# Scattering token numbers in place of token rows in a mixture-of-experts sort that runs beside attention

## The reference, cut to what matters

```python
xn = layernorm(x)
s  = attention(xn)                        # 16 heads of 16, bias by distance (ALiBi)
# mixture of experts, each token goes to 2 of 8 experts
scores   = sigmoid(xn @ router.T)
topk_idx = the two chosen experts, topk_w = their normalised scores
y_e      = (silu(xn @ w_gate[e]) * (xn @ w_up[e])) @ w_down[e]
routed   = sum over the two chosen e of topk_w * y_e
g = silu(routed + shared expert)
out = x + s * g
```

## Time and profile before

| what | us |
|---|---|
| median of 3 runs | 2485.53 |
| lowest and highest of them | 2479.53, 2488.43 |
| the profiled execution | 2477.84 |
| its span from first to last instruction | 2476.1 |
| tokens stage in the span | 0 to 371 |
| attend stage, sort part | 445 to 653 |
| attend stage, expert tiles | 704 to 2043 |
| attend stage, mix | 2047 to 2290 |
| deliver stage | from 2340 |

### The profile page before, as it was taken

How to read it: one execution, slowest core, us unless ns; L and a number is a source line. 1 busy time by engine, 2 the same in 40 slices (tenths; PEclk the granted TensorE clock), 3 DMA queues, 4 the chain that set the end, 5 groups by cost and what they waited for, 6 DMA issues and landing times. The chain is left out here.

```text
span 2476.1 us, 41361 instructions
## 1 busy us (share of the span) xinstructions
PE 2051.5 (83%) x15921; PEld 723.3 (29%) x15922; DVE 1007.1 (41%) x2375; ACT 1792.6 (72%) x2080; POOL 549.8 (22%) x577
## 2 busy tenths in 40 slices
PE   4688875676799999999999999999999998788565
PEld 2345542111122224222222332222224221111154
DVE  6676656411133335333333443333335332444255
ACT  3444444566798888888888888888888887888610
POOL 1222220566401111111111111111111104555022
PEclk9888886878899999999999999999999998989888
DMA  9766664554323325332333443233335323433296
GB/s 305 232 212 215 214 204 110 147 155 143 116 74 92 98 78 142 96 86 84 95 96 85 111 114 98 79 94 92 91 87 136 102 63 81 120 103 105 56 285 219
DMA packets 212584, 316.75 MB, mean 128 GB/s; under 512 B 81744, under 2 KB 156112, under 8 KB 212128
## 3 DMA queue, kind: packets, MB, share of 16 engines
q1 hardware_dynamic: 172064, 197.63, 29.1%
q0 software_dynamic: 31872, 108.03, 14.4%
q10 hardware_dynamic: 8448, 8.39, 1.0%
HBM read 196.25 MB, written 125.83 MB: 130 GB/s over the span
## 5 line engine op out<-in xcount | busy, mean ns | idle before, releaser
L1203 ACT ACTIVATE probs_att<-SC_att 128x1024 f32<-128x1024 f32 (+10 forms) x1776 | 1578.0, 956 | 289.0 <-PE SC_att L1093 205.5
L1116 PE MATMUL O_att<-probs_att,V_att 128*32 128x512 f32 (+6 forms) x8192 | 954.1, 535 | 17.1 <-DVE probs_att L1229 15.8
L1093 PE MATMUL SC_att<-Q_att,K_att 64*128 64x512 f16 (+6 forms) x4332 | 654.9, 341 | 241.1 <-ACT probs_att L1203 168.5
L1229 DVE TENSOR_TENSOR probs_att<-probs_att,decay_att 128x128 f32<-128x128 f32 x1024 | 293.5, 291 | 1094.6 <-ACT probs_att L1203 1012.3
L1093 PEld LDWEIGHTS SC_att<-Q_att,K_att 64*128 64x128 f16 (+1 forms) x4332 | 183.2, 94 | 1138.9 <-ACT probs_att L1203 850.2
L1116 PEld LDWEIGHTS O_att<-probs_att,V_att 128*32 128x32 f32 x8192 | 167.6, 110 | 248.6 <-issue 202.3
L1038 POOL DMA_DIRECT2D ys<-ys_att x72 | 51.5, 716 | 743.3 <-DVE ys_att L1276 743.3
L1033 POOL DMA_DIRECT2D xs_att<-xs x72 | 53.3, 740 | 445.6 <-PE TY_att L1137 431.8
L1045 POOL DMA_INDIRECT rows_in_att<-ys,place x128 | 125.5, 981 | 117.5 <-DVE gate_all L1285 83.5
L581 POOL TENSOR_TENSOR parts_tok<-qk_tok,parts_tok 128x512 f16<-128x512 f32 x64 | 78.6, 1230 | 247.0 <-ACT parts_tok L601 242.3
L1023 POOL DMA_INDIRECT xs<-rows_in_att,place x128 | 124.4, 972 | 39.6 <-issue 39.6
(11 more groups left out here) (153 smaller groups left out, 1333.2 us busy)
## 6 DMA issues: line engine op xcount, KB each, us to landing
K_att<-k_stack SPq DMA_DIRECT2D x128, 256.0 KB
Q_att<-q_stack SPq DMA_DIRECT2D x128, 256.0 KB
xs<-zero_tok SPq DMA_DIRECT2D x36, 512.0 KB, 3.8
xs_att<-xs POOLq DMA_DIRECT2D x72, 256.0 KB, 3.2
ys<-ys_att POOLq DMA_DIRECT2D x72, 256.0 KB, 2.6
k_stack<-parts_tok SPq DMA_DIRECT2D x96, 128.0 KB
q_stack<-parts_tok SPq DMA_DIRECT2D x96, 128.0 KB
x_raw_tok<-in_x SPq DMA_DIRECT2D x16, 512.0 KB, 5.7
```

Source lines behind the costliest of these rows:

```text
L1093: mm = pe.matmul(SC[:, c % SLOTS, at:at + x1 - x0], K[par][side or 0][rows, k * P:(k + 1) * P], Q[par][rows, x0:x1], start=True, stop=True)
L1116: mm = pe.matmul(O[VW * g:VW * (g + 1), par, col:col + width * len(mine)], V[par][:, k, :], spans[:, j0:j0 + BPB * (len(mine) - 1) + 1:BPB ...
L1203: nc.scalar.activation(probs[chunk.step % DEPTH][:, chunk.base:chunk.base + chunk.width], SC[:, c % SLOTS, start:start + chunk.width], ACT ...
L1229: v.tensor_tensor(diag, diag, decay[:, chunk.head, :], ALU.mult).then_inc(faded, 1)
```

## The change

`xs` is gone. In its place stands `order`, one 4-byte number for each of the 18432 slots, filled with zeros by one DMA of 72 KB. POOL scatters token numbers (`ids`, a constant, held as floats) into `order` with the same 128 indirect DMAs by the same `place`, one after the other with no load and no wait between them. When all have landed it loads `order` as 72 rows of 256 and waits on `order_ready`. PE turns the two halves with two transposes at chunk 252 of batch 0 (`ORDER_AT`), and DVE turns the result into integers (`row_of`). Each `load_tile` then gathers its 256 rows straight from `xn` with two indirect DMAs of 128 rows. The first tile moves from 50 to 56 per cent of batch 0 (chunk 264), with the last where it was. The slots that only fill up a list all name token 0; their results aren't read.

```diff
-FF_FROM, FF_TO = 50, 340
+FF_FROM, FF_TO = 56, 340
+ORDER_AT = 252
+        "ids": np.arange(B * S, dtype=np.float32).reshape(NBLK * TT, P).T,
-        zero = r.sb("zero", [P, 1024])
+        zero = r.sb("zero", [P, SLOTS_IN // P])
...
                 sp.wait_ge(zeroed, 1)
+                sp.dma_start(keep["order"].rearrange("(p k) o -> p (k o)", p=P), zero[:]).then_inc(zeros_out, 16)
                 for j in range(NBLK):
-                    for n in range(j * NZ // NBLK, (j + 1) * NZ // NBLK):
-                        sp.dma_start(keep["xs"].rearrange("(p k) d -> p (k d)", p=P)[:, 1024 * n:1024 * (n + 1)], zero[:]).then_inc(zeros_out, 16)
...
-                def sort_rows(j):
-                    pool.wait_ge(rows_loaded[j % 2], 16 * (j // 2 + 1))
-                    for t in range(TT):
-                        for n in range(2):
-                            nc.gpsimd.indirect_dma_start(keep["xs"], index(keep["place"][:, n, j * TT + t:j * TT + t + 1]),
-                                                         rows_in[:, j % 2, t, :], None).then_inc(sorted_out[j % 2], 16)
+                def sort_tile(t):
+                    for n in range(2):
+                        nc.gpsimd.indirect_dma_start(keep["order"], index(keep["place"][:, n, t:t + 1]), ids[:, t:t + 1], None).then_inc(sorted_out, 16)
...
-                    src = keep["xs"][i * TILE_IN:(i + 1) * TILE_IN, :].rearrange("(t p) d -> p t d", p=P)
-                    pool.dma_start(xs[:, i % 2], src).then_inc(xs_in[i % 2], 16)
+                    for t in range(2):
+                        nc.gpsimd.indirect_dma_start(xs[:, i % 2, t, :], None, keep["xn"], index(row_of[:, t, i:i + 1])).then_inc(xs_in[i % 2], 16)
...
-                load_rows(0)
                 pool.wait_ge(routed, 1)
-                for j in range(NBLK):
-                    if j + 1 < NBLK:
-                        if j > 0:
-                            pool.wait_ge(sorted_out[(j + 1) % 2], 16 * 2 * TT * ((j + 1) // 2))
-                        load_rows(j + 1)
-                    sort_rows(j)
-                for n in range(2):
-                    pool.wait_ge(sorted_out[n], 16 * 2 * TT * (NBLK // 2))
+                for t in range(NT):
+                    sort_tile(t)
+                pool.wait_ge(sorted_out, 16 * 2 * NT)
+                pool.dma_start(order[:], keep["order"].rearrange("(i k) o -> i (k o)", k=TILE_IN)).then_inc(order_in, 16)
+                pool.wait_ge(order_ready, 1)
                 load_tile(0)
                 load_tile(1)
...
+                def turn_order():
+                    pe.wait_ge(loaded, 64)
+                    pe.wait_ge(order_in, 16)
+                    for t in range(2):
+                        mm = pe.transpose(TY[:, t * TILES_IN:(t + 1) * TILES_IN], order[:, t * P:(t + 1) * P], ident[0:TILES_IN, 0:TILES_IN])
+                    mm.then_inc(order_turned, 1)
...
                                 prefixes()
+                            if b == 0 and c == ORDER_AT:
+                                turn_order()
...
+                def take_order():
+                    dve.wait_ge(order_turned, 1)
+                    v.tensor_copy(row_of[:].rearrange("p t i -> p (t i)"), TY[:, 0:2 * TILES_IN]).then_inc(order_ready, 1)
...
+                        if b == 0 and c == ORDER_AT:
+                            take_order()
```

More of the change, by code:

```diff
@@ L394, in tokens_stage @@
         ALL_LOADED = 16 * len(loads)
-        NZ = SLOTS_IN * D // 1024 // P
         x_rows = a["x"].rearrange("b s d -> (b s) d")
@@ L467, in _ @@
                 sp.wait_ge(w_stored, 32 * E)
-                sp.wait_ge(zeros_out, 16 * NZ)
+                sp.wait_ge(zeros_out, 16)
                 sp.wait_ge(shift_out, 16 * NBLK)
@@ L853, in attend_stage @@
         O = r.ps("O", [P, 2, TB])
-        rows_in = r.sb("rows_in", [P, 2, TT, D])
+        fetched = r.sb("fetched", [P, 4, 2, D])
+        ids = r.sb("ids", [P, NT])
+        order = r.sb("order", [TILES_IN, TILE_IN])
+        row_of = r.sb("row_of", [P, 2, TILES_IN], I32)
         ident = r.sb("ident", [P, P])
@@ L913, in attend_stage @@
         step, counted = r.sem("step"), r.sem("counted")
-        rows_loaded = [r.sem(f"rows_loaded{n}") for n in range(2)]
-        sorted_out = [r.sem(f"sorted_out{n}") for n in range(2)]
+        sorted_out, order_in, order_turned, order_ready = r.sem("sorted_out"), r.sem("order_in"), r.sem("order_turned"), r.sem("order_ready")
         w_in = [r.sem(f"w_in{n}") for n in range(3)]
@@ L928, in attend_stage @@
         per_choice = lambda t: t.unsqueeze(2).broadcast_to([P, NT, E])
-        route_loads = [(lower[:], a["lower"]), (starts[:], a["starts"]), (lane[:], a["lane"]),
+        route_loads = [(lower[:], a["lower"]), (starts[:], a["starts"]), (lane[:], a["lane"]), (ids[:], a["ids"]),
                        (earlier[:].bitcast(U16), a["earlier"]), (every[:].bitcast(U16), a["every"]),
@@ L935, in attend_stage @@
         weighted = keep["weighted"].rearrange("(n r) s -> n r s", r=HD)
-        pairs = rows_in[:].rearrange("p n t d -> p (n t d)").rearrange("p (n k d) -> p n k d", n=4, d=D)
+        pairs = fetched[:]
         PRODUCTS = [(c, wp, xp) for c in range(DC) for wp, xp in ((0, 0), (0, 1), (1, 0))]
@@ L1011, in _ @@
             def _(pool):
-                rows_of = lambda j: keep["xn"][j * TB:(j + 1) * TB, :].rearrange("(t p) d -> p t d", p=P)
                 index = lambda ap: bass.IndirectOffsetOnAxis(ap=ap, axis=0)
-                def load_rows(j):
-                    pool.dma_start(rows_in[:, j % 2], rows_of(j)).then_inc(rows_loaded[j % 2], 16)
-                def sort_rows(j):
-                    pool.wait_ge(rows_loaded[j % 2], 16 * (j // 2 + 1))
-                    for t in range(TT):
-                        for n in range(2):
-                            nc.gpsimd.indirect_dma_start(keep["xs"], index(keep["place"][:, n, j * TT + t:j * TT + t + 1]),
-                                                         rows_in[:, j % 2, t, :], None).then_inc(sorted_out[j % 2], 16)
+                def sort_tile(t):
+                    for n in range(2):
+                        nc.gpsimd.indirect_dma_start(keep["order"], index(keep["place"][:, n, t:t + 1]), ids[:, t:t + 1], None).then_inc(sorted_out, 16)
                 def load_tile(i):
@@ L1130, in turn_tile @@
                         pe.wait_ge(loaded, 64)
-                    pe.wait_ge(xs_in[i % 2], 16 * (i // 2 + 1))
+                    pe.wait_ge(xs_in[i % 2], 32 * (i // 2 + 1))
                     if i > 0:
@@ L2663, in build @@
             "xn": scratch("xn", (B * S, D), F32),
-            "xs": scratch("xs", (SLOTS_IN, D), F32),
+            "order": scratch("order", (SLOTS_IN, 1), F32),
             "ys": scratch("ys", (SLOTS_IN, D), F32),
```

## The result

The changed kernel takes 2565.1 us, the median of 4 runs (2563.6 to 2583.5), against 2482.9 for the kernel before in the same comparison: a ratio of 1.0331, 95% interval 1.0297 to 1.0365. It is 3.3% slower where I had forecast 0.9% faster, and the time lies beyond my upper end of 2513.

The account below looks back on a forecast made before the run. PE and ACT set the pace in the tiles; in the sort, pauses beside POOL's dense indirect DMAs cost 88 us. Gains 4 + 1 + 18 - 1 = 22 us gave 2456 profiled, 2463 as median; 80% range 2390 to 2513.

Parts of the forecast that it names:

- I take the present share, because the issue rate stays: Sort: attention still loses 42% of the time, now 164.5 us instead of 207.7, a gain of 18 us; chance 0.34.
- The right rival: Sort: an unbroken run of scatters is worse, 2496 us at 62% lost, 2525 at 80%; chance 0.15.
- the one stretch of 16 scatters: Sort, 630.9 to 653 us: the only unbroken stretch, ACT busy 8.3 of 22.1 us, used as the bound of 62% loss.
- the start of the tiles was clean: Tiles' start, 653 to 659 us: three weight gathers and two row loads without a pause, held against bytes as cause.
- the mix's gathers as back to back: Mix: indirect DMAs issued much as in the sort, ACT losing 0.35 us each against the sort's 0.69.
- The pauses go with the bytes: Sort rival: with bytes down 256-fold the 88 us come back, 2393 us, up to 2425; chance 0.28.
- by number: Sort rival: loss follows the number of DMAs or is unrelated to them, the 88 us stay, 2481 us; chance 0.14.
- slow scatters: Sort rival: 4-byte scatters are slow, PE waits at chunk 252, 2541 us at 2.5 us each; 0.09 together with gathers.
- Order: Chunk 252: the wait for the list is covered by 78 us; cost 0 to 4 us, taken as 1.
- Zeros and the row load: Tokens stage: fewer zero writes gain 4 us (bounds 0 and 17); row loads removed gain 1 (0 to 2).
- Tiles: Expert tiles: two gathers replace each direct load, hidden by POOL's waiting; cost taken as 0, upper bound 50 us.
- my other terms: Forecast terms besides the sort's 18 us: zeros gain 4, row loads gain 1, order costs 1, tiles 0.

Follow-up runs that it names:

- b_rows_unbroken: Kernel before with its 1 KB row scatters, the breaks and 14 of the 16 row loads taken out; 2561.8 us in one run.
- d_zeros: `d_fill` with the 36 writes of 512 KB of zeros put back in the tokens' stage, into a spare buffer; 2411.2 us, ratio 0.9748.
- d_direct: `d_fill` with each tile's 256 rows loaded by one direct transfer of consecutive rows instead of two gathers; 2393.8 us, ratio 0.966.
- d_fill: Changed kernel with POOL clearing 1280 columns after each scatter, order turned at chunk 400, tiles from 0.92 batches on; 2399.6 us, ratio 0.9691.
- d_after: The changed kernel unaltered, run and profiled once more in a later comparison; 2559.9 us, ratio 1.0352 to the kernel before.
- e_before_fill: Kernel before with POOL clearing 1280 columns after each of its 128 row scatters, tiles from 0.92 batches on; 2406.8 us, ratio 0.9721.
- e_straight: Changed kernel with 128 direct transfers of the same 512 bytes by POOL in place of the scatters; one run of 2390.4 us.
- e_gathers: Changed kernel with 128 gathers of 4 bytes a row from the list into SBUF in place of the scatters; one run of 2561.5 us.
- after: First profile of the changed kernel, nothing further altered; the kernel's median is 2565.1 us, ratio 1.0331 to the kernel before.

## Why the prediction was wrong

- **The step that failed** is in the sort: "I take the present share, because the issue rate stays". The lost share went from 42% to 97%. It isn't a property of the issue rate alone but of the run: some 5.5 us for each 8 scatters, 1.4 for each 4, nearly all of the time for 128. The 42% were a mean over runs of 8 parted by a landing wait and a row load, and the change removed what parted them. The sort was priced at -18 us; it came out at +77.
- The right rival was on the page with a chance of 0.15, and even it was priced too low, at 80% and 2525 at most. Its best row was mine: in the one stretch of 16 scatters 62% were lost, "its second half is all loss". A stretch that begins free and ends at full loss is no constant share, and it should have been carried on at the share of its second half: all of 164.5 us lost gives 2485.5 + 76.5 - 4 = 2558.
- That bytes don't decide was right (`b_rows_unbroken`), but I misread the row that I gave for it: the start of the tiles was clean since it holds three indirect DMAs in a row, and a run that short costs next to nothing. I took it as a word about bytes only.
- I also read the mix's gathers as back to back, "much the same" as the sort. They are 1.25 us apart in places, but in its first 50 us in runs of 2 to 8 with waits for DVE between, and the earlier trace rows has 126 of them in 240 us. That the mix lost less for each DMA was one more word for the length of the runs; I put it down to the kind of transfer.
- *The pauses go with the bytes*, *by number* and *slow scatters* fell: bytes fell 256-fold and the loss rose, the number was equal, and no wait of PE on the order stood in the changed kernel. Slow landing was real all the same, 10 us where I had reckoned 0.34 for a scatter; unbroken, it only showed once, as the 9.64 us before the list's load.
- **Order:** right. Covered, and POOL then waited 166.9 us for `order_ready`. My "tens of us" was short, since the stall also held PE back from its chunk 252.
- **Zeros and the row load:** I took 5. By the runs' medians the zeros are worth 2411.2 - 2399.6 = 11.5, inside my bounds of 0 and 17 but above what I took. The two intervals touch, though, and `d_zeros` has its first head load at 366.21 where `d_direct`, without the zeros, has it at 365.35 and `d_fill` at 354.38, so the price of the zeros stays open. In the profiles the changed kernel's first head load comes 18.8 us earlier than before (351.89 against 370.64), but `d_after`, the same kernel, has it at 365.23, so one profile isn't enough for a term of this size.
- **Tiles:** I took 0, with 50 as the upper bound. `d_direct` against `d_fill` gives 5.8 us for the 144 gathers, 0.04 each, with intervals that overlap. From the start of batch 1 to that of batch 2 pass 462.8 us before and 471.3 after (467.6 in `d_after`); the two kernels with and without gathers differ there by 1.7 (478.5 and 476.8) and one batch later by 3.0 (477.2 and 474.2). The other few us of that drift, part of it the denser tiles, were not followed up.
- With the fill on both sides the change stands at 0.9691 against 0.9721, 0.3% or 7 us with overlapping intervals, near the 4 us that my other terms sum to. But `e_before_fill` spends 22.5 us on the wait for its first tile, which `d_fill` doesn't have (1.9), so with its tiles later the kernel before could well be the faster one. Whether the change is a gain or a loss by itself is not shown. What is shown is that it took away the breaks that kept a hidden cost down.

The Trainium skill (SBUF — State Buffer, section Who interferes with whom) has it that a DMA never contends with a compute engine and that PE and ACT never wait on anyone. For direct transfers the runs agree (`e_straight`, ACT 89.76 of 100 us), for close runs of indirect DMAs they don't (`e_gathers`, 6.33 of 100). The section is about access to SBUF, and no run shows that the pauses come from there. What the skill says of transfers below 512 bytes (DMA: Bandwidth & Descriptors, Specifications), a read, a change and a write, fits the longer landing of the 4-byte scatters (10.0 us); but the gathers of `e_gathers`, 4 bytes a row too, had landed 1.93 us behind the last. What makes the scatters land late no run isolated.

**Open:** by which path an indirect DMA holds ACT, and PE behind it, up. ACT's pauses carry no releaser in the profile, and no run looked inside. Open too is why one comparison in six had a milder form of it. The fill may act by the time that it takes or by keeping POOL from issuing; the landing waits did the same without any work on POOL, so time between issues is what both have in common. A gap inside a run didn't free the attention, though: POOL issued nothing for the 9.2 us before 578.55, and ACT stood until 578.23; in `d_after` such a gap of 8.4 us let one chunk through.

## What to carry to other kernels

A loss measured as a share of a stretch may depend on how the work in it is parted. Before a change takes a wait away, ask whether that wait was the pause in which others got on, and read how the loss runs inside the longest unbroken piece. Don't issue indirect DMAs from POOL back to back beside work that must go on: parting them by 1.2 us of fill made this kernel 6.3% faster than the changed one and 3.1% faster than the one before. When something is spread out, move what waits for it too: six of these experiments lost 21 to 186 us to a deadline left too early.

## What was unexpected of the hardware

- 128 indirect DMAs 1.26 us apart leave PE and ACT 4 to 13 of 100 us, for rows of 4 bytes or 1 KB, scatter or gather; the granted clock is 0.50 to 0.54 of its upper level in that window, at or near 1.2 GHz, with PE busy 7 to 13 us of it. Parted to 2.42 us they leave ACT 89.
- The pauses are 25 to 30 us long in the changed kernel and end one by one, each letting a single chunk through. Before the same chunks they have nearly the same length in three profiles (`after`, `d_after`, `e_gathers`): 30.17, 30.17 and 30.18 us before one, 29.88 in all three before the next.
- 8 scatters of 128 x 4 bytes take 10.0 us to land, the same with 1 KB mostly 1.7 us; in an unbroken run the issue rate stays at 1.26 us all the same.
- The tokens' stage doesn't have one length: two executions of one kernel have the first head's load at 351.89 and 365.23, with PE busy 260 and 279 us of the first 371 at a granted clock of 0.89 and 0.84; in other kernels with the same stage it lies between (354.38, 357.27, 359.63) or up to 367.26.
